# Expert down projections as three half-precision products, two pairs behind the up projections

## What is computed

```python
up_s = einsum('th,seh->tse', xt, shared_up)
shared = einsum('tse,she->th', gelu(up_s), shared_down)
probs = softmax(xt @ router_w.T)
topk_p, topk_i = top_k(probs, 4)
gate = zeros_like(probs).at[rows, topk_i].add(topk_p)
up_r = einsum('th,reh->tre', xt, routed_up)
act = gelu(up_r) * gate[:, :, None]
routed = einsum('tre,rhe->th', act, routed_down)
return shared + routed
```

## Time and profile before

| | us |
|---|---|
| median of 3 runs | 1245.17 |
| lowest, highest | 1242.21, 1247.08 |
| the profiled execution | 1248.9 |
| its span, first to last instruction | 1247.2 |

### The profile page before, as it was taken

One profiled execution on the slowest core, in us unless ns is written; L12 is line 12 of the kernel. 1 busy time (PEld: TensorE's weight loads), 2 busy tenths in 40 slices (PEclk: granted clock), 3 DMA queues, 4 the chain that ended last, 5 costly groups with the idle time before them and its releaser, 6 DMA issues.

```text
span 1247.2 us, 22856 instructions
## 1 busy us (share of the span) xinstructions
PE 1156.8 (93%) x8404; PEld 958.7 (77%) x8404; DVE 828.3 (66%) x2630; ACT 646.6 (52%) x1363; POOL 152.1 (12%) x184
## 2 busy tenths in 40 slices
PE   3899999889999989999989999988999999999996
PEld 2667888767888867888877788876787878888875
DVE  5634557773657872565875565687788778696663
ACT  2236542325644225654224754276667876958562
POOL 4799404100000000000000000000001000000000
PEclk9999999999999999799999999998989899998988
DMA  8200000100000100000010101120000100001000
GB/s 310 105 18 1 1 1 1 51 18 1 2 2 1 45 25 1 2 1 1 1 35 18 71 2 43 43 68 1 1 18 9 27 13 23 1 27 35 18 10 17
DMA packets 21388, 33.27 MB, mean 27 GB/s; under 512 B 11424, under 2 KB 12192, under 8 KB 20128
## 3 DMA queue, kind: packets, MB, share of 16 engines
q1 hardware_dynamic: 21280, 31.82, 7.5%
HBM read 27.62 MB, written 4.19 MB: 26 GB/s over the span
## 4 chain that ended last, share of the span: by engine, by line
PE 75%; DVE 15%; ACT 6%; issue 2%; POOL 1%; ACTq 0%; DVEq 0%; POOLq 0%
PE ps L506 40%; PE ps L756 6%; PE ps L654 4%; DVE z L1617 2%; PE ps L646 2%; PE ps L644 2%; PE ps L672 2%; PE ps L671 2%; DVE arena L1811 2%; DVE arena L1431 2%; PE ps L670 2%; ACT L1288 1%; PE ps L610 1%; PE ps L701 1%; PE ps L905 1%
## 5 line engine op out<-in xcount | busy, mean ns | idle before, releaser
L506 PE MATMUL ps<-wts,arena 128*128 128x256 f32 (+2 forms) x1008 | 199.8, 354 | 17.9 <-DVE pq L1461 6.5
L506 PE MATMUL ps<-arena,wts 128*128 128x256 f16 (+1 forms) x1344 | 183.0, 289 | 20.6 <-ACTq L479 20.6
L506 PEld LDWEIGHTS ps<-wts,arena 128*128 128x128 f32 (+1 forms) x1008 | 152.2, 153 | 55.7 <-DVE pq L1461 7.5
L506 PEld LDWEIGHTS ps<-arena,wts 128*128 128x128 f16 (+1 forms) x1344 | 150.0, 112 | 46.5 <-issue 20.5
L1617 DVE SCALAR_TENSOR_TENSOR z<-ps,small,z 128x256 f32<-128x256 f32 x256 | 123.9, 484 | 41.3 <-PE ps L756 26.8
L756 PE MATMUL ps<-wts,pq 128*128 128x256 f32 x512 | 120.8, 380 | 6.2 <-DVE z L1617 6.2
L1222 ACT ACTIVATE pq<-ps 128x512 f32<-128x512 f32 x72 | 43.0, 597 | 144.9 <-PE ps L506 144.5
L1502 DVE CUSTOM_DVE_ANT_0 pq<-ps,mb 128x128 f32<-128x128 f32 x128 | 36.8, 287 | 114.0 <-PE ps L646 113.3
L756 PEld LDWEIGHTS ps<-wts,pq 128*128 128x128 f32 x512 | 92.6, 190 | 18.7 <-DVE z L1617 4.9
L1094 ACT ACTIVATE arena<-ps 128x512 f32<-128x512 f32 (+2 forms) x112 | 63.8, 580 | 64.0 <-PE ps L506 47.8
L1288 ACT ACT_TABLE_LOAD x70 | 89.8, 1283 | 1.2
(11 more groups left out here) (286 smaller groups left out, 2375.4 us busy)
## 6 DMA issues: line engine op xcount, KB each, us to landing
cT<-in_cT SPq DMA_DIRECT2D x16, 256.0 KB, 2.7
wts<-in_up SPq DMA_DIRECT2D x1, 2304.0 KB, 15.4
wts<-in_down SPq DMA_DIRECT2D x1, 2304.0 KB, 20.4
xT<-in_xT SPq DMA_DIRECT2D x8, 256.0 KB, 3.7
xin<-in_x SPq DMA_DIRECT2D x8, 256.0 KB, 3.0
xmid<-xin SPq DMA_DIRECT2D x8, 256.0 KB, 2.0
wts<-in_w SPq DMA_DIRECT2D x2, 1024.0 KB, 5.1
wts<-in_c SPq DMA_DIRECT2D x16, 128.0 KB, 3.1
```

Source lines behind the costliest of these rows:

```text
L506: ins = mm(out_, l, r, start=(n == 0), stop=(n == len(pairs) - 1))
```

## The change

The down weights are split as the up weights are, by nine more groups on GpSimd, placed second. Each activation is split too: after Gelu, ScalarE copies it to half precision (`ahalf`, part 0), and GpSimd subtracts that from the activation (part 1, `lows`). TensorE makes three half-precision products for each one of before. Both s run as one stream, and the down projection follows two pairs behind the up projection; activation buffers are four, in a ring over the stream. The output projection of s=1 stands directly behind the last `turn_out`, and the other woven steps are moved by a pair. VectorE waits for `halfv` instead of `halfq` before it writes `z2[1]`; the splits of the last two attention weights come after GpSimd's subtractions of turn 0. The factor 1/16 for the down weights goes into the gates and into the shared sum.

```diff
         def abuf(s, e):
-            i = s * 2 + e // 2 % 2
+            i = (s * NE + e) // 2 % 4
...
+        def ahalf(s, e):
+            i = 4 + (s * NE + e) // 2 % 4
+            return pq[:, i * 2 * T:(i + 1) * 2 * T].bitcast(F16).rearrange("p (i j t) -> p i j t", i=2, j=2)
...
             def expert_down(s, e):
-                eng.wait_ge(*pe.at("up", s, e, "out"))
-                act = abuf(s, e)
+                eng.wait_ge(*pe.at("alo", s, e))
+                act = ahalf(s, e)
+                def pairs(j, t):
+                    return [(act[:, a_, j, t * P:t * P + P], dnh[:, 2 * (e + j):2 * (e + j) + 2, b_, :])
+                            for a_, b_ in THREE]
...
                     for t in range(TT):
-                        ins = mm(o[:, t * C:t * C + C], act[:, j, t * P:t * P + P], down[:, e + j, :],
-                                 start=True, stop=True)
+                        ins = group(o[:, t * C:t * C + C], pairs(j, t))
...
+                eng.wait_ge(*pe.at("halfd"))
                 pe.stage("moe")
-                for s in range(NS):
-                    for e in range(0, NE + 2, 2):
-                        if e < NE:
-                            expert_up(s, e)
-                        if e >= 2:
-                            expert_down(s, e - 2)
...
+                stream = [(s, e) for s in range(NS) for e in range(0, NE, 2)]
+                for i in range(len(stream) + 2):
+                    if i < len(stream):
+                        expert_up(*stream[i])
+                    if i == 0:
+                        for m in range(6, AM, 2):
+                            turn_out(1, m)
+                        out_proj(1)
+                    if i >= 2:
+                        expert_down(*stream[i - 2])
+                    if i == 6:
+                        transposes(1, "zT2", z2[1], ("z2", 1))
+                    if i == 8:
+                        router(1)
...
+                    A(flat(abuf(s, e)), psv(("up", s, e)), ACT.Gelu, scale=1.0 / UPS).then_inc(
+                        *act.up(("up", s, e, "out")))
+                    eng.wait_ge(*act.own())
+                    A(ahalf(s, e)[:, 0], abuf(s, e), ACT.Copy).then_inc(*act.up(("ahi", s, e)))
...
+            def lows():
+                for s in range(NS):
+                    for e in range(0, NE, 2):
+                        hi, lo = (ahalf(s, e)[:, i] for i in range(2))
+                        eng.wait_ge(*po.at("ahi", s, e))
+                        G.tensor_tensor(lo, abuf(s, e), hi, ALU.subtract).then_inc(*po.up(("alo", s, e)))
...
-                    ("halfv", wvv, wvh, ("Vp", NS - 1, TT - 1, 1)), ("halfq", wq, wqh, ("Q", NS - 1, AM - 2)),
...
+                if mark == "halfq":
+                    po.turn = 0
+                    po.stage("low")
+                    lows()
...
-                                eng.wait_ge(*v.at("halfo" if g else "halfq"))
+                                eng.wait_ge(*v.at("halfo" if g else "halfv"))
...
-                            if e == 6:
+                            if e == 8:
                                 moe_low(1)
-                            if e == 10:
+                            if e == 12:
                                 route(1)
-                            if e == 12:
+                            if e == 14:
                                 route2(1)
```

More of the change, by code:

```diff
@@ L736, in expert_down @@
             def expert_down(s, e):
-                eng.wait_ge(*pe.at("up", s, e, "out"))
-                act = abuf(s, e)
-                for j in range(2):
[L740 to L753, removed]
+                eng.wait_ge(*pe.at("alo", s, e))
[3 more added lines that the diff above has]
+                            for a_, b_ in THREE]
+                if e == 0:
+                    o = take(("shared", s), ("shared", s, "out"))
+                    for t in range(TT):
+                        ins = group(o[:, t * C:t * C + C], pairs(0, t) + pairs(1, t))
+                    ins.then_inc(*pe.up(("shared", s)))
+                    return
+                for j in range(2):
                     o = take(("dn", s, e + j), ("dn", s, e + j, "out"))
                     for t in range(TT):
-                        ins = mm(o[:, t * C:t * C + C], act[:, j, t * P:t * P + P], down[:, e + j, :],
-                                 start=True, stop=True)
+                        ins = group(o[:, t * C:t * C + C], pairs(j, t))
                     ins.then_inc(*pe.up(("dn", s, e + j)))
@@ L1216, in _ @@
                 act.stage("moe")
[L1217 to L1226, removed]
-                                    turned(1, m)
-                            if e == 4:
-                                ln_rstd(1, "ln_2", TT)
-                            if e == 8:
-                                moe_in(1)
-                            if e == 12:
-                                gates(1)
+                stream = [(s, e) for s in range(NS) for e in range(0, NE, 2)]
+                for i, (s, e) in enumerate(stream):
+                    eng.wait_ge(*act.at("up", s, e))
+                    if i >= 4:
+                        s4, e4 = stream[i - 4]
+                        eng.wait_ge(*act.at(*(("dn", s4, e4 + 1) if e4 else ("shared", s4))))
+                    A(flat(abuf(s, e)), psv(("up", s, e)), ACT.Gelu, scale=1.0 / UPS).then_inc(
+                        *act.up(("up", s, e, "out")))
+                    eng.wait_ge(*act.own())
+                    A(ahalf(s, e)[:, 0], abuf(s, e), ACT.Copy).then_inc(*act.up(("ahi", s, e)))
+                    if i == 0:
+                        for m in range(6, AM, 2):
+                            turned(1, m)
+                    if i == 3:
+                        ln_rstd(1, "ln_2", TT)
+                    if i == 6:
+                        moe_in(1)
+                    if i == 9:
+                        gates(1)
                 nc.scalar.preload_act_table_set("natural_log_exp_and_others")
@@ L1707, in _ @@
                             eng.wait_ge(*v.at("shared", s))
[L1708 to L1709 removed]
+                            V_.scalar_tensor_tensor(z[s][:, :, :],
+                                                    psv(("shared", s)).rearrange("p (t c) -> p t c", t=TT),
+                                                    1.0 / UPS, z2[s][:, :, :], ALU.mult, ALU.add).then_inc(
+                                *v.up(("shared", s, "out")))
                         else:
@@ L2110, in _ @@
                     eng.wait_ge(*po.reached((0,) + read))
-                if mark == "halfo":
+                if mark == "halfq":
+                    po.turn = 0
+                    po.stage("low")
+                    lows()
+                    po.stage("halves")
+                    po.turn = None
                     eng.wait_ge(*po.reached((0, "shared", NS - 1, "out")))
@@ L2125, in _ @@
                 po.mark(mark)
+            po.stage("low")
+            for g in range(1, TURNS):
+                po.turn = g
+                lows()
+            po.turn = None
             po.stage("layer1")
```

17 lines of the change are left out of this document (3 added, 14 removed).

## The result

| | before | after |
|---|---|---|
| time, median of 8 runs each | 1249.13 us (1242.21 to 1254.09) | 1262.38 us (1258.48 to 1264.61) |
| ratio to before, 95% interval | | 1.0095 (1.0068 to 1.0121) |
| profiled execution, its span | 1248.9, 1247.2 us | 1263.95, 1262.2 us |
| mean granted clock in the profiled execution | 0.969 | 0.949 |

Slower by 0.95%; the forecast was 1243, and 1262 lies above the range of 1232 to 1255. Before itself lay 4 us higher over eight runs than over the three first shown.

The account below looks back on a forecast made before the run. TensorE held 75% of the chain, but VectorE the expert stage's later part in turns 1 and 2. Terms -2.1+1.4+1.4-4.0+1.0 = -2.3 took 1248.9 to 1246.6; less 3.7 to the median's measure, about 1243 us, range 1232 to 1255.

Parts of the forecast that it names:

- rival 4: TensorE's clock falls in the new gap before the next turn, three times: 1.7 us each, +5, 1248; chance 0.06.
- Activations in time: Expert stage: Gelu, copy and subtraction take 4.1 us of 6.55, hidden; only the second sequence's LayerNorm holds TensorE some 0.7 us.
- Output projection 2.1 us after turn_out: Turn 1: output projection, waiting for ScalarE and VectorE, starts at 363.75, turn_out at 361.64; 1.6 us after turn_out's end.
- First routed add at 14 us: Turn 1: VectorE starts its first routed pair at 375.6, 14 us after turn_out; before, at 372.79.
- The turn is VectorE's, so TensorE's 30 us don't show: Turns 1 and 2, expert stage: from the first mix VectorE sets the pace; only -0.6 us a turn before contention.
- Contention 2.0 a turn, all in the first mix: Expert stages: two GpSimd subtractions delay VectorE's first mix, none the second; 2 us, bounds 0 and 7.3.
- Turn 0 -3.1: Turn 0's expert stage: next turn starts at 228.0 instead of 231.08, as weight splitting no longer meets its mixes.
- Routing contention +1.0: Just ahead of turn 0's turn_out: GpSimd's down-weight splitting lies beside the routing of s=0, costing 1.0 us.
- Splits beside turn 1's first stage +1.0: Last two weights' splits move to about 228 to 266, beside turn 1's first stage: +1.0 us, bounds 0 and 3.
- Rival 1: Expert stage: VectorE is not held up by GpSimd; the -14 bound or half, 1231 to 1238; chance 0.28.
- rival 2: Expert stage: TensorE sets the pace all through, full 30 us less output projection waits, 1222; chance 0.06.
- Rival 3: GpSimd's reads push VectorE's mixes, 3.65 us each: +17 bound, 1262, at half of it 1254; chance 0.22.

Follow-up runs that it names:

- experiment 4: Before with TensorE made to wait at the end of turns 0 to 2 for VectorE's last adds: 1.0186; second kernel, 24 busywork matmuls ahead of the wait: 1.0128.
- experiment 1: Before once more: 0.9986; and the changed kernel with unused matmuls on constants at TensorE's stands in the expert stages: 0.9993 to before, median 1249.88 us.
- Experiment 3: Changed kernel without GpSimd's 72 activation subtractions, the third product taking the high part instead of the low: ratio to before 1.0032, median 1254.6 us.
- (c): As (a), but with 30 busywork matmuls at the end of turn 0 and 32 before layer 1: ratio to before 0.9907, median 1241.43 us.
- Experiment 5: Changed kernel once more (1.0080), and four kernels with late output projection plus busywork, two of them with the second mix later: 0.9907 to 0.9950.
- (b): As (a), but the second mix moved behind expert 16's adds in place of the 14 busywork matmuls: ratio to before 0.9929, median 1243.53 us.
- (a): Changed kernel with late output projection, plus busywork of 12 at pair 16 and 14 at a turn's end: ratio to before 0.9950, median 1244.40 us.
- experiment 2: Changed kernel with the output projection of s=1 back behind the first down projection: 0.9952, and on another chip 0.9972; medians 1244.47 and 1244.49 us.

## Why the prediction was wrong

**The step that failed is the rejection of rival 4**, "it stood 4.81 us at 813 and the granted clock stayed 1.00 over that stretch". The row is right and does not speak to the question: it covers the stand, and the fall comes at its end. Before has 0.51 over 818.65 to 822.10, and experiment 4 brings such falls about in before's own code. Rival 4 was also counted too small: at +5 for three gaps, priced by the gap's length, where half clock was 3.4 to 6.8 us long and also came behind turn_out, at the new wait before the output projection, which the prediction had as 1.6 us and for whose clock it never asked. Measured by experiment 1 it is 11.4 us of layer 0, against a term of nothing in the sum. The rest of the way from 1243 to 1262.38 is 4.0 us of before itself, whose median over eight runs is 1249.13 and not 1245.17 (I had taken 3.7 off for a profiled execution that was an ordinary one), and some 3.5 in the other terms: experiment 1's kernel ends layer 0 1.2 us behind before (without its 6.2), forecast 2.3 ahead.

The Trainium skill (TensorE: Matmul & The Clock Gate, "HAM oscillation — how this bites in real kernels") asks for no long idle gaps of TensorE and counts the half clock behind them as a price of its own. The trace after and experiment 4 agree; my only seemed to differ. I had named that rule in the prediction and set it aside for one row.

Step by step:

- *Down projection, 1.31 us, 12 records*: right.
- *Activations in time*: right. The LayerNorm stall was 0.34 us, expected 0.7.
- *Output projection 2.1 us after turn_out*: 2.57 in this trace, with turn_out itself at half clock (1.11 for 0.66), and 2.11 in the second trace of after.
- *First routed add at 14 us*: 16.5, most of it by the half clock of the output projection, 7.40 for 5.40.
- *The turn is VectorE's, so TensorE's 30 us don't show*: right, where the clock stays up. In experiment 1 VectorE begins its first mix 45.2 us after turn_out, as walked (406.8 less 361.64), and the next turn starts 63.05 after it, expected 63.1. That this fits to 0.1 is partly luck, with 3.4 us at half clock behind its turn_out. Turn 3's stage is 62.43 there, 3.8 below before's, expected 4.0. In after turn 3 gave 2.5.
- *Contention 2.0 a turn, all in the first mix*: 2.74, as 1.79 and 0.95. The second mix was not free: a subtraction came into it too. In experiment 1's kernel it is 1.79 and 0.25, 2.04 in all. Experiment 3 shows the cause. (The mix of turn 0 that I read as 7.8 is 7.87, 210.43 to 218.30; the bound moves by 0.1.)
- *Turn 0 -3.1*: -1.5. I had the last two weights' splits begin at 228. They began at 223.67, as soon as GpSimd's last subtraction was done, and lay in the second mix, which took 7.10 us (5.10 in turn 1). GpSimd's timeline, against the earlier trace rows:

```profile
222.43 1.15 POOL L2114 TENSOR_TENSOR pq<-pq 128x512 f16<-128x512 f32 x1 [4.50 <-ACT pq L1228]
223.67 1.81 POOL L2134 TENSOR_SCALAR wts<-wts 128x512 f32<-128x512 f32 x1
225.54 0.85 POOL L2136 CAST z<-wts 128x512 f16<-128x512 f32 x1
```

- *Routing contention +1.0*: the stretch is 1.8 longer. TensorE waits 1.95 before turn 0's turn_out where it waited 0.73, which is 1.2 of it. The clock does not explain it: both traces have 3.4 us at half clock in this stretch, and four kernels with the change that have none there still take 164.7 to 165.9. Where the other 0.6 comes from is not shown.
- *Splits beside turn 1's first stage +1.0*: the stage is 4.9 longer, but 2.75 of it are the 16 projections at half clock (6.47 for 3.72), and another 1.44 are lost to 3.4 us at half clock at 264.3. The 0.7 left is the splits: TensorE waits 2.14 at 263.03 where before it waited 1.44, for a VectorE that spent 1.39 on the instruction of the earlier trace rows which takes 0.69. In after's second trace and in (c) the wait is 1.45, and (c), with the clock up, has 130.57 for the stage, so there the splits cost nothing. VectorE's timeline after:

```profile
260.37 1.39 DVE L1478 TENSOR_TENSOR arena<-arena 128x512 f32<-128x512 f32 x1
```

Rival 1 fell with the mixes, rival 2 with VectorE's waits. Rival 3's full bound was 1262, 1254 at half of it. The measured 1262.38 sits on that bound by luck: full contention meant 7.3 us in the mixes of a turn, and 2.74 were measured.

**What stays open.** Layer 1, untouched by the change, took 427.0 to 438.5 us over the traces here, at a granted clock of 0.93 to 0.90: 428.6 before, 437.2 and 438.5 in the two of after, and 427.0 in experiment 4's second kernel:

```profile
835.70:1262.70 427.00, 402.63 (x2620) 334.71 (x2620) 316.92 (x975) 293.38 (x611) 19.25 (x14) 0.93 0.07 19
```

Experiment 5's (b) has 437.3 and is faster than before all the same, and experiment 4's first kernel, without the change, has 436.1. So part of it is chance of the execution; whether layer 0's stands make a low clock in layer 1 likelier, these single traces can't tell. One kernel's time moves with its clock: the ten runs of (a) go from 1233.81 us at a mean granted clock of 0.973 to 1250.87 at 0.959.

## What to carry to other kernels

When a change frees the engine that held the path, ask where it will now stand, and look at the granted clock of every stand that the trace of before already has, from inside it to some microseconds behind it, not over the stand alone. Price each new stand with the half clock behind it, and then look for the cheapest way to close it: here thirty microseconds taken from the matmuls gave a slower kernel, and the output projection three steps later in the list, which closes a stand and feeds VectorE sooner, brought its ratio from 1.0095 to 0.9952. Matmuls put into the waits gave back some 12 us at the large stands (experiment 1) and nothing that the medians show at the last ones ((a) of experiment 5). And an engine that stands empty is not free to use: here GpSimd's work slowed VectorE's instructions with two inputs from SBUF (the mixes, 5.94 us for 4.15), and the work queued behind it moved up into them as soon as it was done (7.10 us in turn 0).

## What the runs showed of the hardware

- Whether TensorE's clock fell at a stand was certain only for long ones. In layer 0 of the twelve traces here it fell at all 23 stands of 3.4 to 6.3 us, 21 times before the stand was over (by up to 4.3 us), and at 11 of 20 stands of 2.2 to 3.0 us. It also fell 1.0 to 1.5 us behind nine of the 48 stands of 1.30 us in the attention stages, one of them in before's turn 2, at 497.9. Behind the 2.15 us before turn_out in turns 1 to 3 it fell in 14 of 27 turns: none of three in before's trace, but four of six in experiment 4's, whose code is the same there, so before's trace was a lucky one. With a second stand of 1.46 close behind it, in after's two traces and experiment 3's, it fell all nine times. Where it fell behind turn_out alone, 24 ups took up to 4.45 us, 2.78 otherwise. This is (c), turn 1:

```profile
360.52 0.66 PE L708 MATMUL ps<-ident,arena 128*128 128x128 f32 x4 [2.15 <-DVE arena L1536]
361.01 4.45 PE L513 MATMUL ps<-arena,wts 128*128 128x256 f16 x24
```

- One GpSimd subtraction (419.38 to 420.63) held a VectorE instruction on 128x2 elements for a whole microsecond, 1.12 us for 0.15, when it met it in the second mix of experiment 2's kernel. The Trainium skill (SBUF — State Buffer, "Who interferes with whom") has this kind, two SBUF inputs beside a GpSimd reader, as the one that contends; the adds, with one SBUF input beside PSUM, kept 6.54 to 6.55 us per twelve in all the traces.

```profile
418.94 0.68 DVE L1431 TENSOR_TENSOR arena<-xT 128x510 f32<-128x510 f32 x1
419.53 1.12 DVE L1432 TENSOR_TENSOR arena<-xT 128x2 f32<-128x2 f32 x1
```
